# Perceiver block on one core: reordering the first maxima of cross attention

## Chip, cores, metric

One Trainium2 chip, one core. The metric is the device time of one execution in microseconds (us); lower is better.

## What is computed

Three residual layers on x (8 batches, 64 tokens, 512 features). The change touches only the first, cross attention to a context of 1601 tokens per batch:

```python
C_q  = layernorm(x) @ Wq_d                  # 512 tokens x 64
C_kv = ctx @ Wkv_d                          # per batch 1601 x 32 latents
q    = (C_q @ W_qk).reshape(b, n, 16, 32)   # 16 heads
scores = einsum('bnhl,bkl->bhnk', q, C_kv) / sqrt(32)
out = einsum('bhnk,bkhd->bnhd', softmax(scores), (C_kv @ Wv_u).reshape(b, k, 16, 32))
x = x + out
```

The second layer is an attention of 32 heads over gathered cache blocks, the third a gated feed-forward layer whose weights are first quantised. Both come after the cross attention and are not changed.

## The kernel before

Every engine has its own instruction stream; semaphores order them. The streams of the cross attention are written by hand, in order. TensorE is PE, VectorE DVE, ScalarE ACT, GpSimd POOL, and SyncE (SP) issues most transfers.

**Data.** `c_t` holds, for each of three batches in flight, the compressed context with latents on partitions: rows 0 to 31 the rounded high part, 32 to 63 the low part (value minus high), 64 to 95 the high part again. `q_t` holds the queries as high, high, low, so that one matmul over 96 rows gives a product of split precision. A "pair" is two matmuls into two neighbouring PSUM banks (402 keys each): `max_scores(b, i)` makes pair i of batch b (16 pairs: 8 tiles of 128 query rows by two halves of the keys), `take_max(b, i)` on DVE takes the maximum over both banks. After all 16, `negate_max` and `turn_max` put the negated maxima into a row of `q_t`; the scores are then made a second time, transposed (`scores`), exponentiated by ACT (`exponential`), multiplied with the latents (`values`) and summed by POOL (`add_pair`).

**Prologue (0 to 51 us).** The layer norm, the queries of token tiles 0 to 3, the compression of batch 0 (bank 4) and of batch 1 (bank 3), and the 16 maxima of batch 0, for which nothing can run ahead. PE's order is: `compress(0)`, `latent_queries(1)` (C_q of tiles 1 to 3), `natural(0)` (four transposes of batch 0's latents, which wait for DVE's copy `c_parts`), `queries(1)`, then pairs 0 to 15. Behind pairs 2 to 6 stands a chunk of `compress(1)`, behind pair 7 `natural(1)`, behind pairs 8 and 11 `queries(2)` and `queries(3)`.

ACT, in `first_keys`, copies `c_high`, places five pieces of the high part in `c_t`, and copies that part of 32x1601 a second time into rows 64 to 95 (L928, "doubling"). Only then comes `latent_copied(1)`, on which `queries(1)` waits; then the copies of queries 1, the exponential's table and `compressed(1)`, `compressed_high(1)`, and the copies of queries 2 and 3.

DVE subtracts the five low pieces (semaphore `s_kl`, one for each), copies `c_parts`, takes maximum 0, then `place_values(0)` (two copies out of `natural(0)`'s bank), then the maxima 1 to 15, with `place_values(1)` behind maximum 8.

POOL subtracts the low parts of queries 1, makes `c_low` of batch 1, subtracts those of queries 2 and 3 (L613, when ACT's copies L918 are there), fills the row of ones, and goes on to the batches: differences of feed-forward weights (L548), sums of probabilities (L555), and `c_low` of later batches (L569). ACT's exponentials of tile t wait until POOL and PE have read one of four buffers.

SP, in `place_keys(1)`, copies `c_high` and `c_low` of batch 1 by 15 transfers into `c_t`; `max_scores(1, 0)` waits for all of them. In the queue they stand behind the loads of context 2 and of six pieces of feed-forward weights. At the end of the cross attention SP gathers cache blocks and then loads the last weight pieces.

**Banks.** The first pairs of every batch use:

```python
def max_bank(i):
    if i < 2:
        return (6, 4)[i]
    return (4, 6)[i % 2]
```

So pairs 0, 1, 2, 3, 4 use banks 6, 4, 4, 6, 4. Pair 2 waits until maximum 1 is done (`s_max` 2), each later pair i until maximum i - 2 is.

Of the kernel before, what the change touches and what calls it, by code (L numbers as in the profile page):

```python
# [17 lines left out]
ACT = mybir.ActivationFunctionType  # L18
# [13 lines left out]
XH, LQ, LKV, XHD = 16, 64, 32, 32  # L32
NCTX = 1601
# [5 lines left out]
GROUPS = P // LKV  # L39
PER_GROUP = FULL // GROUPS  # L40
MAIN = PER_GROUP * P
SHIFT = 3 * LKV
# [27 lines left out]
def wait(eng, sem, count):  # L70

    if isinstance(count, int) and count <= 0:
        return
    eng.wait_ge(sem, count)
# [241 lines left out]
PIECE_AT = (0, 400, 800, NCTX - PIECE_KEYS)  # L316
PAIRS = PIECES // 2
MAXIMA = PAIRS * QTILES
# [24 lines left out]
CONTEXT_AT = {2: (0,), 3: (1,), 4: (2,), 5: (3,), 6: (DC,)}  # L343


def max_bank(i):


    if i < 2:
        return (6, 4)[i]  # L350
    return (4, 6)[i % 2]


# [8 lines left out]
def cross_attention(core, w, own):  # L362
# [15 lines left out]
    ones, c_nat, c_t, max_row, q_t, wv_u = (w[k] for k in ("ones", "c_nat", "c_t", "max_row", "q_t", "wv_u"))  # L378
# [42 lines left out]
    s_kh = core.sem("first_keys_high_done", own)  # L421
    s_kl = core.sem("first_keys_low_done", own)
# [3 lines left out]
    s_max = core.sem("max_part_done", own)  # L426
# [59 lines left out]
    with nc.Block() as block:  # L486
# [145 lines left out]
        def _(pe):  # L632
            def compress(b, parts=range(DC + 1)):
                bank = COMPRESS_BANK[b]
                if parts[0] == 0:
                    if b == 1:
                        pe.wait_ge(s_cqsb, 2)
                    elif b == 2:
                        pe.wait_ge(s_max, MAXIMA * (b - 1) + 1)
                    elif b > 2:  # L640
                        pe.wait_ge(s_max, MAXIMA * (b - 1) - 1)
                    if b > 0:
                        pe.wait_ge(s_ctx[b % 2], 16 * (b // 2 + b % 2))
                for c in parts:
                    if b == 0 and c < DC:
                        pe.wait_ge(s_ctx0[c], 16)
                    for g in range(GROUPS if c < DC else 0):
                        pe.matmul(psum[g * LKV:(g + 1) * LKV, bank, 0:MAIN], w["wkv_d"][:, c, :],
                                  ctx_t[b % 2][:, c, g * MAIN:(g + 1) * MAIN], start=(c == 0), stop=(c == DC - 1))
                if parts[-1] == DC:  # L650
                    for c in range(DC):
                        for g in range(GROUPS):
                            mm = pe.matmul(psum[g * LKV:(g + 1) * LKV, bank, MAIN:C_WIDTH], w["wkv_d"][:, c, :],
                                           ctx_t[b % 2][:, c, FULL * P:NCTX], start=(c == 0), stop=(c == DC - 1))
                    mm.then_inc(s_c, 1)

            def natural(b):
                bank = NATURAL_BANK[b]
                pe.wait_ge(s_cp, b + 1)
                if b == 1:  # L660
                    pe.wait_ge(s_cnat, 1)
                for i in range(PER_GROUP):
                    pe.transpose(psum[:, bank, i * P:(i + 1) * P], c_parts[:, i * P:(i + 1) * P], core.ident[:, :])
                pe.transpose(psum[0:TAIL, bank, MAIN:MAIN + LKV], c_parts[0:LKV, MAIN:C_WIDTH],
                             core.ident[0:LKV, 0:LKV]).then_inc(s_nat, 1)

            def max_scores(b, i):
                qt, pair = divmod(i, PAIRS)
                bank = max_bank(i)
                if i == 0 and b == 0:  # L670
                    pe.wait_ge(s_kl, GROUPS + 1)
                    pe.wait_ge(s_kh, GROUPS + 2)
                elif i == 0:
                    pe.wait_ge(s_ct, 16 * C_COPIES * b)
                if i == 0:
                    pe.wait_ge(s_qhi, 2 * (b // 2 + 1))
                    pe.wait_ge(s_qlo[b > 1], 2 * (b // 2 if b > 1 else 1))
                    wait(pe, s_shift, b)
                elif i == 1 and b == 0:
                    pe.wait_ge(s_cp, 1)  # L680
                elif i == 1 and b == 1:
                    pe.wait_ge(s_max, MAXIMA - 1)
                elif i == 1:
                    pe.wait_ge(s_d, 2 * (b - 1))
                elif i == 3 and b == 1:
                    pe.wait_ge(s_cnat, 3)
                elif i == 3 and b > 1:
                    pe.wait_ge(s_mix, b - 1)
                else:
                    pe.wait_ge(s_max, MAXIMA * b + (2 if i == 2 else i - 1))  # L690
                for k in range(2):
                    at = PIECE_AT[2 * pair + k]
                    mm = pe.matmul(psum[:, bank + k, 0:PIECE_KEYS],  # L693
                                   q_t[0:SHIFT, b, 2 * qt:2 * qt + 2, :].rearrange("p h n -> p (h n)"),
                                   c_t[0:SHIFT, b % 3, at:at + PIECE_KEYS], start=True, stop=True)
                mm.then_inc(s_sa, 1)
# [68 lines left out]
            def latent_queries(k):  # L765

                a, b = ((0, 1), (1, TT))[k]
                pe.wait_ge(norm.s_exact, b)
                pe.wait_ge(s_wq, 2 * 16)
                for c in range(DC):  # L770
                    for r in range(2):
                        mm = pe.matmul(psum[r * LQ:(r + 1) * LQ, LATENT_BANK[k], 0:(b - a) * P], wq_d[:, c, :],
                                       xn_t[:, c, a * P:b * P], start=(c == 0), stop=(c == DC - 1))
                mm.then_inc(s_cq, 1)

            def queries(j):

                pe.wait_ge(s_cqsb, 1 if j == 0 else 2)
                if j == 0:
                    pe.wait_ge(s_twice, 2)  # L780
                if j == 1:
                    pe.wait_ge(s_qhi, 2)
                    pe.wait_ge(s_qlo[0], 2)
                elif j == 2:
                    pe.wait_ge(s_qraw, 1)
                elif j == 3:
                    pe.wait_ge(s_cp, 2)
                    pe.wait_ge(s_cnat, 2)
                for h in range(0, XH // 2, 2):
                    for r in range(2):  # L790
                        rows = slice(r * LQ, (r + 1) * LQ)
                        mm = pe.matmul(psum[:, QUERY_BANK[j] + r, h // 2 * P:(h // 2 + 1) * P],
                                       w_qk[rows, h:h + 2, :, :], cq_t[rows, j * P:(j + 1) * P], start=True, stop=True)
                mm.then_inc(s_q, 1)
# [7 lines left out]
                norm.tile_turn(pe, j)  # L802
            compress(0)
            latent_queries(1)
            natural(0)
            queries(1)
            for i in range(MAXIMA):
                max_scores(0, i)
                if i in CONTEXT_AT:
                    compress(1, CONTEXT_AT[i])  # L810
                if i == 7:
                    natural(1)
                if i in QUERIES_AT:
                    queries(QUERIES_AT[i])
# [45 lines left out]
        def _(act):  # L860
# [42 lines left out]
            def latent_copied(k):  # L903
                a, b = ((0, P), (P, TOK))[k]
                act.wait_ge(s_cq, k + 1)
                act.activation(cq_t[:, a:b], psum[:, LATENT_BANK[k], 0:b - a], ACT.Copy).then_inc(s_cqsb, 1)
# [14 lines left out]
            def first_keys():  # L921

                act.wait_ge(s_c, 1)
                act.activation(c_high[:, :], psum[:, COMPRESS_BANK[0], 0:C_WIDTH], ACT.Copy).then_inc(s_chi, 1)
                for rows, bank, cols, keys in key_pieces():
                    act.activation(c_t[0:LKV, 0, keys], psum[rows, bank, cols], ACT.Copy).then_inc(s_kh, 1)
                act.wait_ge(s_kh, GROUPS + 1)
                act.activation(c_t[2 * LKV:SHIFT, 0, 0:NCTX], c_t[0:LKV, 0, 0:NCTX], ACT.Copy).then_inc(s_kh, 1)  # L928

            act.dma_start(wq_d[:, :, :], arg["Wq_d"].rearrange("p (c q) -> p c q", c=DC)).then_inc(s_wq, 16)  # L930
            act.dma_start(w_qk_in[:, :, :], arg["W_qk"].rearrange("q (h l) -> q h l", l=LKV)).then_inc(s_wq, 16)
# [5 lines left out]
            for j in range(1, TT):  # L937
                norm.tile_exact(act, j)
            first_keys()
            latent_copied(1)  # L940
            queries_high(1)
            queries_copied(1)
            act.wait_ge(s_rest, 1)
# [28 lines left out]
        def _(dve):  # L972
            def take_max(b, i):
                qt, pair = divmod(i, PAIRS)
                bank = max_bank(i)
                dve.wait_ge(s_sa, MAXIMA * b + i + 1)
                if i == 0:
                    wait(dve, s_neg, b)
                dve.tensor_reduce(max_part[:, qt, pair:pair + 1], psum[:, bank:bank + 2, 0:PIECE_KEYS],  # L979
                                  AX.XY, ALU.max).then_inc(s_max, 1)  # L980
# [73 lines left out]
            dve.tensor_copy(c_parts[:, :], psum[:, COMPRESS_BANK[0], 0:C_WIDTH]).then_inc(s_cp, 1)  # L1054
            for i in range(MAXIMA):
                take_max(0, i)
                if i == 0:
                    place_values(0)
                if i == 8:
                    place_values(1)  # L1060
# [920 lines left out]
```

## Time and profile before

| what | value |
|---|---|
| three runs | 909.49, 909.55, 912.41 us; median 909.55 us |
| the profiled execution | 912.59 us, of which its span is 910.7 us |
| PE busy | 866.1 us, 95% of the span |

The profile shows one execution. A row of the timeline gives start and duration in us from the span's start, engine, source line, output and input tiles, shapes and a count; in brackets stands the idle time of that engine ahead of it and what ended it. PEclk, and the column after the busy times in a row of stretches, is the clock granted to TensorE, 1.00 being 2.4 GHz and 0.50 being 1.2 GHz.

### The profile page before, as it was taken

The page shows a single profiled execution, that of the slowest core. Times are in us where ns is not written, and L with a number is a line of the kernel's source. Part 1 is how long each engine was busy: PE and PEld are TensorE (multiplying, and loading weights), DVE is VectorE, ACT ScalarE, POOL GpSimd, SP SyncE. Part 2 cuts the span into 40 slices and gives each one's busy share as a digit, 9 for nine tenths or more (in the row PEclk, how much of TensorE's full clock was granted, in tenths as well). Part 3 has the DMA queues.
Part 4 walks back from the last instruction along what each step waited for, and adds up shares of the span by engine and source line. Part 5 has one row for each costly group of instructions (what it writes and reads, how often), then busy time and mean ns, then how long its engine had stood idle before and what let it go on. Part 6 is the DMA issues. An engine that isn't in the chain of part 4 may idle for free.

```text
span 910.7 us, 15512 instructions
## 1 busy us (share of the span) xinstructions
PE 866.1 (95%) x5402; PEld 656.5 (72%) x5402; DVE 609.3 (67%) x994; ACT 521.5 (57%) x1010; POOL 416.2 (46%) x272
## 2 busy tenths in 40 slices
PE   6789999999997989999999999999999999899998
PEld 4444555455442668888888888888888887788886
DVE  4665666576551538858587585876858769768884
ACT  4555666666674547636366373763637647555552
POOL 2397887788876015424244242442424524154430
PEclk9979999999998889999999999999999999999999
DMA  9747664623660721102011020110202003445531
GB/s 365 273 173 290 234 244 145 257 89 113 186 202 1 277 82 47 47 1 70 23 46 46 0 69 23 48 44 8 72 12 67 14 1 113 165 139 189 197 101 47
DMA packets 43202, 102.96 MB, mean 113 GB/s; under 512 B 7954, under 2 KB 13074, under 8 KB 42258
## 3 DMA queue, kind: packets, MB, share of 16 engines
q1 hardware_dynamic: 42866, 102.06, 32.6%
q8 instruction: 30, 0.49, 0.2%
q10 hardware_dynamic: 288, 0.26, 0.1%
q14 instruction: 18, 0.15, 0.1%
HBM read 96.95 MB, written 1.05 MB: 108 GB/s over the span
## 4 chain that ended last, share of the span: by engine, by line
PE 60%; DVE 2%; ACT 1%; DMA 1%; POOL 0%; SPq 0%; issue 0%
PE psum L1356 11%; PE psum L1342 10%; PE psum L1472 8%; PE psum L1410 8%; PE psum L1368 6%; PE psum L1486 4%; PE psum L1395 3%; PE psum L1386 3%; PE psum L1391 3%; PE psum L1377 1%; PE psum L1387 1%; PE psum L1389 1%; DMA ffn_raw<-in_L_ffn_mean_w_dram 1%; POOL ffn_quant L1857 0%; DVE x L1828 0%; DVE norm_stats L162 0%
## 5 line engine op out<-in xcount | busy, mean ns | idle before, releaser
L1844 POOL TENSOR_TENSOR head_probs<-head_probs,inverse_den 128x576 f32<-128x576 f32 x128 | 147.3, 1151 | 273.2 <-DVE inverse_den L1697 273.1
L979 DVE TENSOR_REDUCE max_part<-psum 128x1 f32<-128x804 f32 x128 | 121.2, 990 | 48.3 <-PE psum L693 48.2
L869 ACT ACTIVATE probs<-psum 128x512 f32<-128x512 f32 (+1 forms) x208 | 107.8, 601 | 56.5 <-PE psum L714 48.6
L1579 ACT ACTIVATE head_probs<-psum,neg_max 128x576 f32<-128x576 f32 x128 | 94.7, 740 | 51.2 <-DVE neg_max L1710 50.4
L555 POOL TENSOR_TENSOR prob_sums<-probs 128x1024 f32<-128x1024 f32 x48 | 114.0, 2383 | 19.5 <-ACT probs L869 10.5
L1710 DVE TENSOR_REDUCE neg_max<-psum 128x1 f32<-128x576 f32 x128 | 96.9, 757 | 23.9 <-PE psum L1356 22.7
L1356 PE MATMUL psum<-k_high,query_t_high 128*128 (+1 forms) x256 | 86.7, 339 | 2.0 <-DVE coeff L1783 2.0
L1690 DVE TENSOR_TENSOR probs_t_low<-psum,probs_t_high 128x512 fp32r<-128x512 f32 x124 | 84.8, 684 | 1.0
L714 PE MATMUL psum<-q_t,c_t 97*128 97x512 f32 (+1 forms) x208 | 74.2, 437 | 8.7 <-ACT probs L869 7.0
L693 PEld LDWEIGHTS psum<-c_t,q_t 96*128 96x128 f32 x256 | 43.9, 191 | 50.9 <-DVE max_part L979 29.3
L693 PE MATMUL psum<-c_t,q_t 96*128 96x402 f32 x256 | 75.0, 376 | 5.6 <-DVE max_part L979 3.9
L1368 PE MATMUL psum<-ident,head_probs 128*128 128x128 f32 x496 | 77.9, 273 | 1.6 <-DVE query_t_low L1669 1.4
L1857 POOL TENSOR_TENSOR ffn_quant<-ffn_raw 128x1536 f32<-128x1536 f32 x13 | 45.6, 3508 | 67.6 <-DVE ffn_w_low L1774 26.9
L1356 PE MATMUL psum<-k_high,query_t_low 128*128 (+1 forms) x256 | 76.2, 298 | 0.0
L1356 PE MATMUL psum<-k_low,query_t_high 128*128 (+1 forms) x256 | 76.1, 297 | 0.0
L1585 ACT ACTIVATE probs_t_high<-psum 128x512 fp32r<-128x512 f32 x124 | 72.9, 588 | 0.5 <-PE psum L1377 0.5
L1368 PEld LDWEIGHTS psum<-ident,head_probs 128*128 128x128 f32 x496 | 60.6, 140 | 11.4 <-issue 2.2
L714 PEld LDWEIGHTS psum<-q_t,c_t 97*128 97x128 f32 (+1 forms) x208 | 38.4, 192 | 32.1 <-ACT probs L869 23.0
L1593 ACT ACTIVATE wo_t_high<-wo_nat 128x512 fp32r<-128x512 f32 x32 | 20.0, 626 | 72.4 <-PE psum L1410 72.4
L727 PE MATMUL psum<-probs,c_nat 128*32 128x512 f32 (+1 forms) x416 | 61.0, 621 | 0.0
L1752 DVE TENSOR_TENSOR x<-psum,x 128x512 f32<-128x512 f32 x32 | 22.1, 690 | 46.0 <-PE psum L1410 46.0
L548 POOL TENSOR_TENSOR w_raw<-w_raw 128x896 f32<-128x896 f32 x24 | 50.5, 2105 | 4.3 <-DMA w_raw<-in_L_ffn_mean_w_dram 4.3
(221 smaller groups left out, 1924.3 us busy)
## 6 DMA issues: line engine op xcount, KB each, us to landing
ctx_t_odd<-in_ctx_dram SPq DMA_DIRECT2D x4, 3202.0 KB, 10.7
w_raw<-in_L_ffn_w_dram SPq DMA_DIRECT2D x24, 448.0 KB, 5.3
w_raw<-in_L_ffn_mean_w_dram SPq DMA_DIRECT2D x24, 448.0 KB, 6.4
ffn_raw<-in_L_ffn_w_dram SPq DMA_DIRECT2D x42, 256.0 KB, 3.9
ffn_raw<-in_L_ffn_mean_w_dram SPq DMA_DIRECT2D x42, 256.0 KB, 4.2
cache<-in_ctx_dram SPq DMA_DIRECT2D x3, 3202.0 KB, 10.6
wq_nat<-in_L_attn_wq_dram SPq DMA_DIRECT2D x32, 256.0 KB, 2.9
wo_nat<-in_L_attn_wo_dram SPq DMA_DIRECT2D x32, 256.0 KB, 2.7
```

The costliest lines, as they stand in the source:

```text
L555: pool.tensor_tensor(sums[u][:, :], prob_buffer(b, 2 * u)[:, :], prob_buffer(b, 2 * u + 1)[:, :], ALU.add).then_inc(s_add, 1)
L693: mm = pe.matmul(psum[:, bank + k, 0:PIECE_KEYS], q_t[0:SHIFT, b, 2 * qt:2 * qt + 2, :].rearrange("p h n -> p (h n)"), c_t[0:SHIFT, b % 3, ...
L714: pe.matmul(psum[0:rows_of(t), n % SCORE_BANKS, :], lhs, rhs[:, half * BANK:(half + 1) * BANK], start=True, stop=True).then_inc(s_sb, 1)
L869: act.activation(prob_buffer(b, t)[0:rows, half * BANK:(half + 1) * BANK], psum[0:rows, n % SCORE_BANKS, :], ACT.Exp, scale=XSCALE).then_i ...
L979: dve.tensor_reduce(max_part[:, qt, pair:pair + 1], psum[:, bank:bank + 2, 0:PIECE_KEYS], AX.XY, ALU.max).then_inc(s_max, 1)
L1342: mm = pe.matmul(psum[:, head_bank(i), :], wq_t[a][:, c, :], (xh, xl)[b][:, c, :], start=(k == 0), stop=(k == 3 * DC - 1))
L1356: mm = pe.matmul(psum[:, bank, 0:HALF], q_t[a][:, qt * P:(qt + 1) * P], (k_high, k_low)[b][:, keys], start=(step == 0), stop=(step == 2))
L1368: mm = pe.transpose(bank[:, t * P:(t + 1) * P], probs[:, qt, t * P:(t + 1) * P], core.ident[:, :])
L1579: act.activation(probs[:, qt, :].rearrange("p (a k) -> p a k", a=2), psum[:, 2 * (qt % 2):2 * (qt % 2) + 2, 0:HALF], ACT.Exp, bias=neg_max ...
L1690: dve.tensor_tensor(probs_t[1][:, 0:ST, qt * P:(qt + 1) * P], psum[:, turn_bank(qt), :].rearrange("p (t q) -> p t q", t=ST), probs_t[0][:, ...
L1710: dve.tensor_reduce(neg_max[:, qt:qt + 1], psum[:, 2 * (qt % 2):2 * (qt % 2) + 2, 0:HALF], AX.XY, ALU.max, negate=True).then_inc(s["max"], 1)
L1844: pool.tensor_tensor(probs[:, qt, :], probs[:, qt, :], rden[:, qt:qt + 1].to_broadcast([P, KEYS]), ALU.mult).then_inc(s["norm"], 1)
```

## The change

Four things, all in the prologue.

1. For batch 0 all pairs alternate banks 6 and 4, so pair 2 shares banks with pair 0 and waits for maximum 0 alone (`s_max` 1). The last pair now sits in bank 4, hence the wait of `max_scores(1, 1)` for all 16 maxima.
2. ACT copies the latents' queries (`latent_copied(1)`) before the doubling, and doubles in two halves: columns 0 to 801, then 802 to 1600. Pair 0 waits for the first half and three of the five low pieces (keys 0 to 1151; it reads 0 to 801); pair 1 waits for the second half.
3. On PE, `natural(0)` moves from ahead of `queries(1)` to behind pair 1.
4. On DVE, `place_values(0)` moves from behind maximum 0 to behind maximum 2.

```diff
-def max_bank(i):
+def max_bank(b, i):
-    if i < 2:
-        return (6, 4)[i]
+    if b == 0 or i < 2:
+        return (6, 4)[i % 2]
     return (4, 6)[i % 2]
...
             def max_scores(b, i):
                 qt, pair = divmod(i, PAIRS)
-                bank = max_bank(i)
+                bank = max_bank(b, i)
                 if i == 0 and b == 0:
-                    pe.wait_ge(s_kl, GROUPS + 1)
+                    pe.wait_ge(s_kl, GROUPS - 1)
                     pe.wait_ge(s_kh, GROUPS + 2)
...
                 elif i == 1 and b == 0:
+                    pe.wait_ge(s_kh, GROUPS + 3)
                     pe.wait_ge(s_cp, 1)
                 elif i == 1 and b == 1:
-                    pe.wait_ge(s_max, MAXIMA - 1)
+                    pe.wait_ge(s_max, MAXIMA)
...
-                    pe.wait_ge(s_max, MAXIMA * b + (2 if i == 2 else i - 1))
+                    pe.wait_ge(s_max, MAXIMA * b + (2 if i == 2 and b > 0 else i - 1))
...
             latent_queries(1)
-            natural(0)
             queries(1)
             for i in range(MAXIMA):
                 max_scores(0, i)
+                if i == 1:
+                    natural(0)
...
                 act.wait_ge(s_kh, GROUPS + 1)
-                act.activation(c_t[2 * LKV:SHIFT, 0, 0:NCTX], c_t[0:LKV, 0, 0:NCTX], ACT.Copy).then_inc(s_kh, 1)
+                latent_copied(1)
+                for cols in (slice(0, 2 * PIECE_AT[1] + 2), slice(2 * PIECE_AT[1] + 2, NCTX)):
+                    act.activation(c_t[2 * LKV:SHIFT, 0, cols], c_t[0:LKV, 0, cols], ACT.Copy).then_inc(s_kh, 1)
...
             first_keys()
-            latent_copied(1)
             queries_high(1)
...
             for i in range(MAXIMA):
                 take_max(0, i)
-                if i == 0:
+                if i == 2:
                     place_values(0)
```

(`PIECE_AT[1]` is 400, `GROUPS` 4; `take_max` calls `max_bank(b, i)` too.)

## Rows read from the trace of the kernel before

**Rows 1.** The page: busy time of the engines and PE's granted clock by fortieths.
```profile
PE 866.1 (95%) x5402; PEld 656.5 (72%) x5402; DVE 609.3 (67%) x994; ACT 521.5 (57%) x1010; POOL 416.2 (46%) x272
...
PEclk9979999999998889999999999999999999999999
```

**Rows 2.** Timeline, 19 to 30 us: start, duration, engine, line, tiles, count, idle before.
```profile
19.29 2.80 PE L772 MATMUL psum<-xn_t,wq_d 128*64 128x384 f32 x16
...
22.01 1.54 ACT L928 ACTIVATE c_t<-c_t 32x1601 fp32r<-32x1601 f32 x1
...
23.57 0.49 ACT L906 ACTIVATE cq_t<-psum 128x384 f32<-128x384 f32 x1
...
23.62 0.55 PE L663 MATMUL psum<-ident,c_parts 128*128 128x128 f32 x3 [1.53 <-DVE c_parts L1054]
...
24.27 1.16 PE L792 MATMUL psum<-cq_t,w_qk 64*128 64x128 f32 x16
...
25.36 0.99 PE L693 MATMUL psum<-c_t,q_t 96*128 96x402 f32 x4
...
26.03 0.99 DVE L979 TENSOR_REDUCE max_part<-psum 128x1 f32<-128x804 f32 x1 [2.46 <-PE psum L693]
26.94 0.55 DVE L992 COPY c_nat<-psum 128x384 f32<-128x384 f32 x1
...
27.50 0.98 DVE L979 TENSOR_REDUCE max_part<-psum 128x1 f32<-128x804 f32 x1
...
28.54 0.64 PE L693 MATMUL psum<-c_t,q_t 96*128 96x402 f32 x2 [2.19 <-DVE max_part L979]
...
29.10 0.85 PE L648 MATMUL psum<-ctx_t_odd,wkv_d 128*32 128x384 f32 x8
...
29.89 0.63 PE L693 MATMUL psum<-c_t,q_t 96*128 96x402 f32 x2
```

**Rows 3.** Groups of instructions with shapes kept apart, 18 to 51 us.
```profile
L926 ACT ACTIVATE c_t<-psum 32x384 fp32r<-32x384 f32 x4 | 1.9, 478 | 0.1
```

**Rows 4.** Timeline of the later maxima, and two half-clock stretches with their granted clock.
```profile
34.10 0.63 PE L693 MATMUL psum<-c_t,q_t 96*128 96x402 f32 x2
...
43.70 3.70 DVE L979 TENSOR_REDUCE max_part<-psum 128x1 f32<-128x804 f32 x4 [0.58 <-PE psum L693]
...
30.44:33.85 3.41, 3.41 (x19) 0.90 (x18) 1.88 (x2) 0.67 (x2) 3.41 (x2) 0.50 1.04 296
...
47.50:57.74 10.24, 8.81 (x34) 5.47 (x38) 8.32 (x9) 4.73 (x8) 10.04 (x5) 0.50 0.85 329
```

**Rows 5.** Timeline and waits around the first scores of batch 0, all engines.
```profile
41.86 2.04 ACT L918 ACTIVATE prob_sums<-psum 32x1024 f32<-32x1024 f32 x2
...
44.07 9.29 POOL L613 TENSOR_TENSOR q_t<-prob_sums,q_t 32x1024 fp32r<-32x1024 f32 x4 [4.88 <-ACT prob_sums L918]
...
61.05 1.15 POOL L569 TENSOR_TENSOR c_low<-c_parts,c_high 128x449 fp32r<-128x449 f32 x1 [0.20 <-ACT c_high L883]
...
68.64 7.07 POOL L555 TENSOR_TENSOR prob_sums<-probs 128x1024 f32<-128x1024 f32 x3
...
PE psum L714 <- ACT probs L869: 1.3, 2, 0.9
```

**Rows 6.** DMA issues with their time to landing, and issues of the key copies.
```profile
ctx_t_odd<-in_ctx_dram SPq DMA_DIRECT2D x1, 3202.0 KB, 19.6
...
37.93 3.09 SPq L481 DMA_DIRECT2D c_t<-c_high  x4
...
47.40 0.59 SPq L483 DMA_DIRECT2D c_t<-c_low  x1
...
52.99 0.87 PE L693 MATMUL psum<-c_t,q_t 96*128 96x402 f32 x2
```

**Rows 7.** SyncE's and GpSimd's timeline at the start of the last batch.
```profile
234.36 0.36 SPq L284 DMA_DIRECT2D cache<-in_L_attn_k_cache_dram  x1
...
264.84 2.09 POOL L548 TENSOR_TENSOR w_raw<-w_raw 128x896 f32<-128x896 f32 x1 [4.27 <-DMA w_raw<-in_L_ffn_mean_w_dram]
```

More of the change, by code:

```diff
@@ L974, in take_max @@
                 qt, pair = divmod(i, PAIRS)
-                bank = max_bank(i)
+                bank = max_bank(b, i)
                 dve.wait_ge(s_sa, MAXIMA * b + i + 1)
```

## The prediction

> **What bounds the kernel now.** I read the page first. PE is busy 95% of the span, and the places where it is not, or where its clock is low, are few; the first three fortieths, which hold the prologue, are among them [rows 1]. The chain that ended last runs through PE in nearly all of its length. So a microsecond taken from the prologue counts in full if PE's stream behind it can follow, and that is the question.
>
> Then the timeline of the prologue, for what ends each wait. Three things hold up the maxima of batch 0 [rows 2]. ACT makes the 1.54 us doubling before the 0.49 us copy of the latents' queries, though PE had delivered those at 22.09 (19.29 + 2.80); `queries(1)` starts only at 24.27, behind `natural(0)`, and pair 0 at 25.36. Next, DVE puts the placing of the values between maxima 0 and 1, so maximum 1 starts at 27.50. Then pair 2, which shares its banks with pair 1, waits for that maximum: PE stands idle for 2.19 us until 28.54. Soon after that the clock falls to half for 3.41 us [rows 4].
>
> Last, what follows the prologue, in the timeline and the waits of batch 0. POOL begins its low parts of queries 2 and 3 at 44.07, when ACT's copy of queries 2 (41.86 + 2.04 = 43.90) is there, and is then busy almost without a gap until 75.71 (68.64 + 7.07). Its one wait in between that I use is 0.20 us at 61.05, for ACT's `c_high` of batch 2, which comes from PE. PE waits 1.3 us in all behind ACT, where ACT waits for POOL to free buffers [rows 5]. Here POOL sets the time and PE is hardly ahead of it, so both must move for the end to move.
>
> **The change, part by part.** All starts are those of the trace; hand-overs between engines take 0.06 us (maximum 1 ends at 27.50 + 0.98 = 28.48, pair 2 starts at 28.54) [rows 2].
>
> *Latents first, `natural(0)` away.* The latents' copy starts at 22.15 and ends at 22.64. `queries(1)` starts at 22.70, and the next instruction of PE can follow 1.09 us later (24.27 to 25.36) [rows 2]: pair 0 at 23.79 in place of 25.36, 1.57 us earlier. The weaker wait on the low pieces costs and gives nothing, because DVE's low pieces are done before pair 0 in either order.
>
> *Doubling in halves.* A 384-column copy takes 0.48 us [rows 3] and the 1601-column one 1.54 [rows 2], which makes 0.87 ns for a column and 0.84 us for each half. The first half runs 22.64 to 23.48, under `queries(1)`, with 0.3 us to spare. The second ends at 24.32. Pair 1 could start at 23.79 + 0.56 (the pitch of a pair, 28.54 to 29.10 [rows 2]) = 24.35 and starts at 24.38. A second instruction costs ACT about 0.14 us (0.84 twice against 1.54), and ACT has `queries(1)` to wait for anyway. If a half took as long as the whole, pair 0 would slip by 0.4 us; if the halves cost nothing extra, nothing changes. Bounds 0 and -0.4.
>
> *Banks alternate, two steps moved.* Maximum 0 starts 0.67 us after its pair (25.36 to 26.03) [rows 2], at 24.46, and ends at 25.45. `natural(0)`, whose first three and last transposes take 0.65 us (23.62 to 24.27), now stands behind pair 1 and fills 24.94 to 25.59; so it is nearly free, since pair 2 could not start before 25.51. Pair 2 starts at 25.59 in place of 28.54: **2.95 us earlier**. A chunk of `compress(1)` takes 0.79 (29.10 to 29.89) [rows 2]; its context lands at 4.30 + 19.6 = 23.9, before it is wanted at 26.15 [rows 6]. Pair 3 starts at 26.94, pair 4 at 28.29, pair 5 at 29.64, by 1.35 us each.
>
> DVE's pitch of maxima is 0.92 us (four in 3.70, the last 0.99 long [rows 4]): maxima 1 and 2 start at 25.38 and 26.30, the values' placing at 27.22, maximum 3 at 27.78 (placing 0.56, from 26.94 to 27.50 [rows 2]). It ends at 28.77, and pair 5, which needs it, comes at 29.64. So the moved placing is hidden behind the chunks of compression; without those it would cost its 0.56 again. What waits for it is `natural(1)`, behind pair 7, far off. The order of ACT's later copies is unchanged.
>
> *The clock.* Before, from pair 3 to pair 5 passed 4.21 us (29.89 to 34.10) [rows 2, 4] where two steps of 1.35 make 2.70: **1.51 us** go to the stretch at half clock, 1.2 GHz, which began after an idle gap of 2.19 us. After the change PE has no gap over 0.1 us from 22.70 on, by the steps above. I take this stretch as gone: pair 5 moves by 34.10 - 29.64 = 4.46 us, that is 2.95 + 1.51. Bounds for this term: 0 and 1.51.
>
> The Trainium skill (TensorE: Matmul & The Clock Gate, "What's actually happening") says that the window in which activity is judged runs freely and does not start with the kernel. By that rule the 1.51 us need not be in every execution before, and the sum for an execution without it would be 2.95.
>
> *From pair 5 to the scores.* Here nothing is edited. The last four maxima are one block on DVE (43.70 to 47.40 [rows 4]) and move by 4.46 as well. POOL's start at 44.07 hangs on `queries(2)` behind pair 8 and moves with it, to 39.61. The rank of waits stays: POOL's stream to 75.71 sets the time.
>
> *Batch 0.* PE runs at half clock from 47.50 to 57.74 [rows 4], around the thin work of the turned maxima. That thin place remains and the low stretch with it, but where it lies against the work is open. PE has no margin where POOL waits for `c_high` (0.20 us at 61.05), so if PE comes later there, POOL does too; if it comes earlier, at most 0.2 us is won, since POOL binds. I take 0.2 us off. Bounds: +0.2, and -1.7 for a low stretch longer by the 3.41 us of the other one, at half speed.
>
> *Transfers.* `place_keys(1)` is issued 37.93 to 47.99, and pair 0 of batch 1 at 52.99 needs it [rows 6]. It moves 4.46 earlier, to 33.47, when the weight loads are still in flight. At worst the transfers land as late as before, 47.99 plus some 2 us (the pace of their issue bounds it from below), against a need at 48.53: PE waits 1.5 us, of which 1.3 are the PE margin against POOL [rows 5]. I take nothing; bound -0.3 to -1.5.
>
> The Trainium skill (DMA: Bandwidth & Descriptors, "Queues, rings and completion order") says that each DMA engine takes descriptors in ring order. By that rule the early key copies do stand behind the weights, and the sum would be smaller by up to that bound.
>
> *The other batches.* They repeat their own periods. The last batch starts on POOL behind a weight transfer (264.84 after 4.27 us of waiting), which follows the gather begun at 234.36 [rows 7]; the gather in turn is released by the batch before it, so this chain moves too.
>
> **Sum.** 2.95 + 1.51 - 0.2 = 4.3 us. The profiled execution took 912.59 us in all (1.89 outside its span), and becomes 908.3. It lies 3.0 us above the median of the runs shown; the median becomes 909.55 - 4.3 = **905.3 us**.
>
> **Rivals.**
>
> 1. *Order alone.* The low stretch at 30 us is absent from the executions that make the median, or another takes its place. For it: the runs shown spread over 3 us with one program, which something of this kind must explain. Against: the idle gap of 2.19 us stands in every execution, by dependencies. 909.55 - 2.95 = 906.6.
> 2. *Given back in batch 0.* PE gets through `compress(2)` later against POOL, by 1.7 us of half clock or 1.5 us of waiting for the keys. 4.3 - 1.6 = 2.7, or 1.1 with both: 906.9 to 908.5. For it: the margin of 0.20 us. Against: a stretch of 10.24 us is already paid.
> 3. *It does not arrive.* A chain of its own, such as transfers, fixes the end of the cross attention: 909.5. For it: POOL waits 4.27 us for a transfer in the last batch. Against: that chain starts from work of batch 5.
> 4. *Slower.* The half clock in batch 0 becomes longer. Each 3.41 us more costs PE 1.7. To pass 912.3 it has to eat 4.3 and then 2.7 more: over 14 us of added low clock beyond what stands at 47.50 to 57.74. Price 912.5 or more. PE is dense from 53 us on, which speaks against it.
> 5. *More.* The later drops of the clock, in the middle of the span [rows 1], fall better as well: one stretch of 3.41 us fewer gives 1.7, so 903.6.
>
> **How the numbers follow.** My forecast 0.50 (its own range 904.7 to 906.0), rival 1 0.18, rival 2 0.13, rival 3 0.07, rival 4 0.04, rival 5 0.08. A change of 0.3% (2.7 us) is about what a measurement of this kernel can tell from none. Faster by more: forecast, rival 5 and nearly all of rival 1 (906.6 is just below 906.8), with a tenth of rival 2: 0.50 + 0.08 + 0.17 + 0.01 = 0.76. Slower 0.04. Within: 0.20. Range 903.4 to 908.4: it leaves out rivals 3 and 4 and the ends of 2 and 5.
>
> **What would show it.** Pair 0 at about 23.8 and pair 2 at 25.6, with no idle PE between; the placing of values between maxima 2 and 3; granted clock 1.00 from 24 to 40 us; POOL's run of low parts starting near 39.6; the last maximum ending near 42.9; PE's first scores near 46 to 46.5; then the same rows as before in the batches, 4.3 earlier. Wrong would be: PE idle at pair 1 for the second half; a half-clock stretch before 35 us; POOL waiting over 1 us for `c_high` of batch 2, or pair 0 of batch 1 waiting for key copies.

## The result: 4.7 to 5.8 us faster, a little more than forecast

In 12 runs each, the changed kernel takes 903.75 us in the median (901.39 to 905.64) and the kernel before 908.81 (905.17 to 914.0). The ratio is 0.9936 with a 95% interval of 0.9919 to 0.9952, which is 5.8 us less, 4.4 to 7.4. (The medians above are 5.1 us apart; the ratio on record is not their quotient, 0.9944, but holds it in its interval.) Measured a second time the ratio is 0.9948 (0.9931 to 0.9964), 4.7 us less, 3.3 to 6.3. The forecast was 4.3 us less, 905.3 us: right in sign, but just short of the first interval. The time measured lies below the range of the forecast itself (904.7 to 906.0), just inside the wide one (from 903.4), and nearest to the price of rival 5, 903.6.

The page of the changed kernel, by the same two rows as [rows 1]:

```profile
PE 861.6 (96%) x5402; PEld 654.4 (73%) x5402; DVE 609.3 (68%) x994; ACT 521.6 (58%) x1011; POOL 416.4 (46%) x272
...
PEclk9989999999998989999999999999999999999999
```

Its timeline of all engines, for [rows 2, 4, 5] (start, duration, engine, line, tiles, count, idle time before):

```profile
18.00 2.80 PE L773 MATMUL psum<-xn_t,wq_d 128*64 128x384 f32 x16
...
20.91 0.49 ACT L908 ACTIVATE cq_t<-psum 128x384 f32<-128x384 f32 x1 [0.23 <-PE psum L773]
21.43 1.63 ACT L932 ACTIVATE c_t<-c_t 32x802 fp32r<-32x802 f32 x2
...
21.46 1.16 PE L793 MATMUL psum<-cq_t,w_qk 64*128 64x128 f32 x16 [0.66 <-ACT cq_t L908]
...
22.55 1.21 PE L694 MATMUL psum<-c_t,q_t 96*128 96x402 f32 x4
...
23.22 2.80 DVE L982 TENSOR_REDUCE max_part<-psum 128x1 f32<-128x804 f32 x3 [0.96 <-PE psum L694]
...
24.27 0.64 PE L694 MATMUL psum<-c_t,q_t 96*128 96x402 f32 x2
...
25.94 0.55 DVE L995 COPY c_nat<-psum 128x384 f32<-128x384 f32 x1
...
26.50 0.98 DVE L982 TENSOR_REDUCE max_part<-psum 128x1 f32<-128x804 f32 x1
...
28.32 0.63 PE L694 MATMUL psum<-c_t,q_t 96*128 96x402 f32 x2
...
37.91 3.70 DVE L982 TENSOR_REDUCE max_part<-psum 128x1 f32<-128x804 f32 x4 [0.58 <-PE psum L694]
...
38.28 9.29 POOL L613 TENSOR_TENSOR q_t<-prob_sums,q_t 32x1024 fp32r<-32x1024 f32 x4 [4.88 <-ACT prob_sums L920]
...
41.94 2.02 PE L702 MATMUL psum<-ident,max_row 128*97 128x128 f32 x8 [1.45 <-DVE max_row L988]
...
55.32 1.14 POOL L569 TENSOR_TENSOR c_low<-c_parts,c_high 128x449 fp32r<-128x449 f32 x1 [0.27 <-ACT c_high L885]
```

Read it from the projection of the latents' queries (18.00; before 19.29). That start differs by 1.29 us for a reason outside the change. The first input was used 0.45 us earlier (3.92 against 4.37), the transposes behind it took 2.59 us in place of 2.82, and `compress(0)` took 2.79 in place of 3.39, first before and then after:

```profile
15.51 3.39 PE L648 MATMUL psum<-cache,wkv_d 128*32 128x384 f32 x32
```

```profile
14.83 2.79 PE L648 MATMUL psum<-cache,wkv_d 128*32 128x384 f32 x32
```

So subtract the start everywhere. Pair 0 starts 4.55 us behind the projection, before 6.07 [rows 2]: 1.52 gained, forecast 1.57. DVE takes three maxima in a row from 23.22, then places the values at 25.94. Pair 2 starts 6.27 behind, before 9.25: 2.98 gained, forecast 2.95. Pair 5 (28.32) is 10.32 behind, before 14.81 [rows 4]: 4.49, forecast 4.46. PE has no bracket, that is no idle gap, between 21.46 and pair 5. POOL's part (38.28) and the last four maxima (37.91) moved by the same 4.50, and POOL's wait for `c_high` at 55.32 is 0.27 us, as before within 0.07.

Two stretches of it, with the granted clock in the third column from the right:

```profile
20.00:42.00 22.00, 18.06 (x159) 10.09 (x155) 18.74 (x27) 17.34 (x22) 9.56 (x5) 1.00 0.96 324
42.00:60.00 18.00, 16.80 (x116) 9.50 (x117) 11.40 (x13) 9.54 (x18) 17.53 (x9) 0.72 0.55 205
```

From 20 to 42 us the clock is 1.00 throughout: the stretch at half clock near 30 us is gone. In the second row it is 0.72, from the stretch at half clock from 41.8 to 52.1 us that replaced the one from 47.50 [rows 4].

### The profile page after: what moved, and what is told of

It reads as the page before. It is cut to its first block, busy times and chain, and to the rows that moved or that the text cites. A ratio compares the mean times of both kernels' runs of the same rounds, so it can differ in the third digit from the quotient of the medians.

```text
span 901.8 us, 15515 instructions
## 1 busy us (share of the span) xinstructions
PE 861.6 (96%) x5402; PEld 654.4 (73%) x5402; DVE 609.3 (68%) x994; ACT 521.6 (58%) x1011; POOL 416.4 (46%) x272
## 4 chain that ended last, share of the span: by engine, by line
PE 61%; DVE 2%; ACT 1%; DMA 1%; POOL 0%; SPq 0%; issue 0%
PE psum L1359 11%; PE psum L1345 10%; PE psum L1475 9%; PE psum L1413 8%; PE psum L1371 6%; PE psum L1489 4%; PE psum L1398 3%; PE psum L1389 3%; PE psum L1394 3%; PE psum L1380 1%; PE psum L1392 1%; PE psum L1390 1%; DMA ffn_raw<-in_L_ffn_mean_w_dram 1%; POOL ffn_quant L1860 0%; DVE x L1831 0%; DVE norm_stats L162 0%
## 5 line engine op out<-in xcount | busy, mean ns | idle before, releaser
L548 POOL TENSOR_TENSOR w_raw<-w_raw 128x896 f32<-128x896 f32 x24 | 50.7, 2111 | 3.6 <-DMA w_raw<-in_L_ffn_mean_w_dram 3.5
```

## The experiments

The start of that projection varies between executions, 16.75 to 19.29 us, whatever the kernel. Inputs are not the main reason: in the profiles that start at 18.20 us or earlier `compress(0)` takes 2.79 us, in those from 18.84 on 3.18 to 3.56. In the traces the first record of full clock comes at 11.63 us where the start is 16.75 and at 16.79 where it is 19.29, so a clock that rises late at the very start would explain it; no run tested that. The table therefore gives, for one profile of each kernel, the distance from that projection (128x384) to the start of maximum 5 and to PE's first matmul for the denominators of batch 0, both in us, and the half-clock stretches before 70 us. The ratio to the kernel before, with its interval, comes from the timed runs.

| kernel | max 5 | denominators | half clock | ratio |
|---|---|---|---|---|
| before | 15.48 | 67.38 | 30.4-33.9, 47.5-57.7 | |
| before, again | 16.79 | 69.15 | 28.4-35.3, 48.9-59.2 | 1.0005 (0.9986-1.0024) |
| before, third | 13.95 | 65.60 | 42.3-52.6 | |
| before, fourth | 15.46 | 67.25 | 29.8-33.2, 46.8-57.1 | |
| after | 10.99 | 62.93 | 41.8-52.1 | 0.9936 (0.9919-0.9952) |
| after, again | 11.06 | 62.70 | 39.6-49.8 | 0.9948 (0.9931-0.9964) |
| early start only | 15.43 | 67.81 | 25.8-32.7, 46.3-56.5 | 0.9986 (0.9968-1.0004) |
| banks only | 12.49 | 64.52 | 43.0-53.2 | 0.9977 (0.9957-0.9996) |
| before, gap filled | 13.95 | 65.59 | 42.8-53.1 | 0.9982 (0.9960-1.0004) |
| after, values back | 11.67 | 64.02 | 42.5-52.8 | 0.9938 (0.9925-0.9950) |
| after, one doubling | 11.47 | 63.55 | 44.2-54.5 | 0.9956 (0.9935-0.9976) |
| after, gap | 17.63 | 70.14 | 27.1-37.3, 51.0-61.2 | 1.0009 (0.9992-1.0026) |
| after, gap filled | 14.04 | 66.40 | 47.2-57.4 | 0.9981 (0.9962-1.0000) |
| after, matrix later | 10.99 | 63.01 | 43.5-53.8 | 0.9959 (0.9946-0.9972) |
| after, warm | 10.98 | 64.14 | 47.6-54.4 | 0.9952 (0.9934-0.9970) |
| warm, ones early | 10.99 | 65.75 | 50.7-57.5 | 0.9979 (0.9964-0.9993) |
| warm, ones early, matrix later | 10.99 | 62.84 | 55.4-62.2 | 0.9947 (0.9927-0.9968) |
| warm, ones early, matrix at end | 10.98 | 61.60 | 46.3-49.7 | 0.9945 (0.9924-0.9966) |

### The two halves of the change

Early start alone takes parts 2 and 3 of the change, with `max_bank`, the wait of pair 2 and `place_values(0)` as before.

> Only the earlier start: latents' queries first, the doubling in halves, natural order behind pair 1; the banks and the place of the values as before. My sum: pair 0 starts 1.57 us earlier against the latent projection's end, maximum 0 ends at the equivalent of 25.45, the values are placed, maximum 1 follows, and pair 2 starts 1.56 us earlier than before. PE still idles about 1.4 us before pair 2. If the idle gap of 2.2 us was what brought the half clock near 30 us, it may or may not come with 1.4: gain 1.6 without the clock term, 3.1 with it. Rival (a start fixed by something else, a transfer): gain 0.

Banks alone is the rest:

```diff
-    if i < 2:
+    if b == 0 or i < 2:
...
-                if i == 0:
+                if i == 2:
                     place_values(0)
```

> Only the banks alternate and the values are placed behind maximum 2; the start as before. My sum: pair 0 as before, pair 2 starts when maximum 0 ends, 27.08 by the trace of before in place of 28.54, so 1.4 to 1.5 us earlier. PE idles 0.7 us before it. Gain 1.4 if the half clock near 30 us stays, 2.9 if it goes. Rival (the placing of the values holds later maxima back): gain under 1.

Pair 2 of the early start, on PE's timeline, and its stretch of half clock:

```profile
24.82 0.64 PE L694 MATMUL psum<-c_t,q_t 96*128 96x402 f32 x2 [1.64 <-DVE max_part L982]
...
25.80:32.70 6.90, 6.90 (x34) 2.11 (x30) 3.04 (x4) 1.82 (x3) 4.67 (x2) 0.51 1.03 352
```

Pair 2 of the kernel with banks alone:

```profile
24.91 0.64 PE L693 MATMUL psum<-c_t,q_t 96*128 96x402 f32 x2 [0.73 <-DVE max_part L979]
```

Pair 2 starts 7.90 us behind the projection in the first (24.82 - 16.92) and 7.77 in the second (24.91 - 17.14), against 9.25 before: 1.35 and 1.48 gained, and both together 2.98 in the changed kernel. They nearly add up (2.83). But PE still stands idle for 1.64 us in the first, half clock follows 1.0 us after pair 2 starts, and at maximum 5 nothing is left of the gain. In the second the gap is 0.73 us and none follows in this profile. The two ratios, 1.3 and 2.1 us of gain, have intervals too wide to tell them apart.

### The clock

Seven unused matmuls behind pair 1 of the kernel before, and nothing else:

```diff
                 max_scores(0, i)
+                if i == 1:
+                    for _ in range(7):
+                        pe.matmul(psum[:, 3, 0:PIECE_KEYS], ..., c_t[0:SHIFT, 0, 0:PIECE_KEYS], start=True, stop=True)
```

> The kernel before, with seven more matmuls of 96x402 into bank 3 behind pair 1, whose results nobody reads, so that PE works in the gap of 2.2 us and nothing else moves. Clock theory: the half clock near 30 us is gone and with it 1.5 us, gain 1.5. Rival (the stretch of half clock is chance, or hidden behind other waits): gain 0, or a loss of 0.2 where the fill runs over the gap.

```profile
23.89 1.46 PE L811 MATMUL psum<-c_t,q_t 96*128 96x402 f32 x7
26.24 0.64 PE L693 MATMUL psum<-c_t,q_t 96*128 96x402 f32 x2 [0.89 <-DVE max_part L983]
...
28.94 0.63 PE L693 MATMUL psum<-c_t,q_t 96*128 96x402 f32 x2
```

The fill (L811) leaves 0.89 us of the 2.19 us gap, pair 2 stays where it was (9.23 behind the projection), no half clock comes before 42 us, and pair 4 follows at the pace of 1.35 us for each. The measured ratio is 1.6 us of gain, with an interval that just reaches zero. The mean granted clock of the timed runs, which the record has for each of them, says the same with less doubt: 0.9849 in the 12 runs with the fill, 0.9815 in the 35 of the kernel before beside them. Read as time at half clock, (1 - 0.9849) x 2 x 905 us, that is 27 against 34 us in a run.

The kernel before was profiled three more times.

> The kernel before against itself, for how far two sets of its runs differ and how its half-clock stretches and its start vary between executions. Ratio 1.000; if the extra in the changed kernel's result came from a start 1.3 us earlier and from shorter half-clock stretches after 275 us by chance, this profile too will show other values there than the first one did.

> The kernel before, a third profile. Clock theory: half clock begins within 4 us of pair 2's idle gap, for 3.41 or 6.83 us, and the distance from the projection of the latents' queries to the denominators of batch 0 is 67.4 us with one step, about 69 with two. Chance theory: in some profile there is none, and the distance is 65.8.

> As the third profile of the kernel before: half clock behind the gap for 3.41 or 6.83 us; distance 67.4 or 69 us.

The second profile of the kernel before, and the third with its pair 2:

```profile
28.40:35.30 6.90, 6.90 (x34) 2.12 (x30) 3.02 (x4) 1.60 (x3) 4.68 (x2) 0.51 1.00 313
```

```profile
25.99 0.64 PE L693 MATMUL psum<-c_t,q_t 96*128 96x402 f32 x2 [2.19 <-DVE max_part L979]
...
20.00:42.00 22.00, 16.94 (x152) 9.90 (x152) 16.12 (x22) 14.35 (x17) 7.85 (x4) 1.00 0.92 323
```

So with the same gap of 2.19 us, of four executions one had 6.83 us of half clock behind it, two had 3.41, and one had none. Against the third, whose maximum 5 comes at 13.95 like that of the filled kernel, the others lose 1.5 us with one step and 2.8 with two, and at the denominators 1.7 and 3.6. My expectation that every profile would have one fell; it was made from two profiles. The Trainium skill (TensorE: Matmul & The Clock Gate, "What's actually happening") says that the window of the clock's monitor runs freely, so the placing varies from run to run. By that rule the stretch need not be the same each time; the traces agree, with 0, 3.41, 3.41 and 6.83 us.

The converse, in the changed kernel: pair 2 waits for ACT's copies of queries 1, with a bare gap and with ten unused matmuls in it.

```diff
+                elif i == 2 and b == 0:
+                    pe.wait_ge(s_max, 1)
+                    pe.wait_ge(s_qraw, 1)
```

> The changed kernel with one more wait: pair 2 waits for ACT's copies of queries 1 (which end at 27.21 in the trace after), so PE idles about 2.9 us between natural order and pair 2 where it had no gap. Clock theory: the direct loss is 3.0 us up to pair 2, and a half-clock stretch of one or two steps of 3.41 us follows within 4 us of the gap and costs another 1.5 to 2.8, so 4.5 to 5.8 later than the changed kernel at maximum 5 and after. Rival (a low stretch is chance): 3.0 later, no stretch.

> The same wait, but ten more matmuls of 96x402 into bank 3 stand ahead of it, whose results nobody reads, so PE works through the gap. Clock theory: 3.0 us later than the changed kernel at maximum 5, with the granted clock at 1.00 up to 40 us. The difference to the kernel with the bare gap is the price of the clock alone, 1.5 to 2.8 us. Rival: both the same.

Pair 2 of the kernel with the bare gap, and its stretch:

```profile
28.56 1.01 PE L697 MATMUL psum<-c_t,q_t 96*128 96x402 f32 x2 [3.11 <-ACT prob_sums L923]
...
27.10:37.30 10.20, 8.74 (x36) 2.82 (x40) 4.02 (x6) 2.79 (x4) 4.67 (x2) 0.50 1.01 333
```

The same stretch with the gap filled:

```profile
27.10:37.30 10.20, 9.03 (x92) 4.13 (x92) 6.81 (x9) 3.72 (x6) 5.68 (x3) 1.00 1.02 345
```

The filled kernel is 3.05 us later than the changed one at maximum 5 (14.04 against 10.99), as expected. The fill does not close the gap: 1.06 us of it are left. The bare gap costs 3.59 us more there and 3.74 at the denominators. Its half clock is 10.2 us long, one step of 3.41 more than I allowed, and begins at 27.1, inside the gap. In time the ratios differ by 0.0028, 2.5 us, but their intervals overlap. The mean granted clock of the ten timed runs each is 0.9811 with the bare gap and 0.9854 with the filled one, 34 against 26 us at half clock. The work is the same but for the fill, so it is the idle time of PE that brings the half clock here. In the profiles it costs 3.7 us on top of the wait, in the times 2.5 with a wide margin.

The gaps ahead of pair 2 can be ranked over the profiles. Behind 0.73 us (banks only), 0.89 (before, gap filled) and 1.06 (after, gap filled) no half clock came before 42 us; with 1.64 (early start only) it was 6.9 us, with 2.19 (before, four profiles) 0, 3.41, 3.41 and 6.83, with 3.11 (after, gap) 10.2. Most of these are single profiles, and no limit can be read from them.

### The small parts

> The changed kernel once more, for a second interval beside the first (0.9936, 0.9919 to 0.9952). The additive account (2.96 us of order, 1.6 us of clock, the mean of what the runs with filled and unfilled gaps gave) makes 4.6 us, ratio 0.9950. A further cause in the change would keep it at 0.9936 or lower. In the profile no half clock between 20 and 40 us; the later stretches, after 270 us, elsewhere than in the first profile.

It came out at 0.9948, near the 0.9950 of the sum and inside the first interval.

Values back puts `place_values(0)` behind maximum 0 again.

```diff
-                if i == 2:
+                if i == 0:
                     place_values(0)
```

> The changed kernel with the placing of the values back behind maximum 0. Maximum 1 then ends 0.56 us later, and pair 3, which waits for it, is ready at 26.98 against 26.94 by my sum. So nothing: 0 to 0.2 us lost at maximum 5, ratio as the changed kernel. Rival (this move carries a large part of the gain): 0.5 us or more lost.

```profile
24.35 0.85 PE L648 MATMUL psum<-ctx_t_odd,wkv_d 128*32 128x384 f32 x8 [0.61 <-DMA ctx_t_odd<-in_ctx_dram]
```

The ratio is that of the changed kernel (0.9938). In the profile maximum 5 is 0.68 us later, but 0.61 of it is this wait: `compress(1)` waits for the context of batch 1 itself, which I had counted as landed well ahead. In this execution the projection started early (16.82) and the context landed at 24.3. The changed kernel has come within reach of that transfer. The wait also hides what the move itself would cost:

```profile
23.10 0.64 PE L694 MATMUL psum<-c_t,q_t 96*128 96x402 f32 x2
...
23.68 1.88 DVE L982 TENSOR_REDUCE max_part<-psum 128x1 f32<-128x804 f32 x2
```

Pair 3 could follow pair 2 by 1.35 us, at 24.45, but maximum 1 ends at 23.68 + 0.98 = 24.66. So pair 3 would come at 24.72, 0.27 us late, where my sum had 0.04. This is an estimate; no run shows it bare. At the denominators this profile is 1.09 us later (64.02 against 62.93), which the ratio does not confirm.

One doubling joins the two halves of ACT's copy, and pair 1's wait for the second half goes.

```diff
-                    pe.wait_ge(s_kh, GROUPS + 3)
...
-                for cols in (slice(0, 2 * PIECE_AT[1] + 2), slice(2 * PIECE_AT[1] + 2, NCTX)):
+                for cols in (slice(0, NCTX),):
```

> The changed kernel with the doubling in one instruction of 1.54 us behind the latents' copy. Pair 0 waits for all of it: the copy ends at 22.64 by the trace of before and the doubling at 24.18, so pair 0 starts at 24.24 in place of 23.79, 0.45 us later, pair 1 right behind it at 24.80 in place of 24.38. All later pairs 0.4 us later. Rival (the halves carry nothing, later waits absorb it): 0.

```profile
24.32 0.97 PE L693 MATMUL psum<-c_t,q_t 96*128 96x402 f32 x4 [0.45 <-issue]
```

PE stands 0.45 us before pair 0, and maximum 5 is 0.48 later (11.47 against 10.99). As expected; the ratios cannot resolve it.

### What binds in batch 0

The forecast held that POOL binds there and PE could win 0.2 us at most. Warm adds eleven unused matmuls (`keep_warm(n)` issues n of those of the fill, into bank 0):

```diff
+                if i in (13, 15):
+                    pe.wait_ge(s_qraw, 2)
+                    keep_warm({13: 2, 15: 5}[i])
             turn_max(0)
+            keep_warm(4)
```

> The changed kernel with eleven more matmuls into bank 0, whose results nobody reads: two behind pair 13, five behind pair 15, four behind the turned maxima. They fill PE's gaps from 38 to 45 us. If the half clock from 41.8 to 52.1 goes, PE's turned maxima take 1.1 us in place of 2.0 and its scores and compression of batch 2 come up to 5 us earlier. By my reading POOL binds from 38 to 68 us: the third sum of probabilities then ends no more than 0.3 us earlier, and the kernel gains 0.3 at most. Rival (PE binds in batch 0, through its low clock): gain 2 to 5 us.

DVE, then PE, then two stretches of the warm kernel:

```profile
41.30 1.21 DVE L1040 TENSOR_SCALAR diag<-ident,cos_col 128x128 f32<-128x128 f32 x1
42.43 2.41 DVE L1041 TENSOR_SCALAR swap<-swap,sin_col 128x128 f32<-128x128 f32 x1
44.88 2.37 DVE L1043 TENSOR_TENSOR rope<-diag,swap 128x128 f32<-128x128 f32 x1
...
47.61 1.90 DVE L991 TENSOR_REDUCE max_part<-psum 128x1 f32<-128x804 f32 x2
...
48.66 5.35 PE L648 MATMUL psum<-cache,wkv_d 128*32 128x384 f32 x32 [1.76 <-DVE max_part L991]
...
40.80:47.50 6.70, 4.85 (x23) 3.23 (x22) 6.55 (x7) 5.10 (x8) 6.58 (x4) 1.00 0.87 301
47.60:54.40 6.80, 5.74 (x56) 2.20 (x60) 1.90 (x3) 0.00 (x0) 6.72 (x3) 0.50 0.57 245
```

The fill does its work: 1.00 up to 47.5, and the first score comes 26.26 us behind the projection in place of 27.16. Then PE waits 1.76 us for maximum 0 of batch 1. On DVE that maximum stands behind the rotation matrix (41.30 to 47.6), whose 128x128 instructions take up to 2.4 us beside POOL's. The wait is itself a gap, the clock falls to half inside it, at 47.6, and the compression of batch 2 takes 5.35 us. The denominators are 1.2 us later than without the fill, and no gain is measured over the changed kernel. Neither POOL nor PE's clock alone explains that: a third engine holds PE.

With POOL's fill of the row of ones also moved ahead of the low parts of queries 2:

```diff
                     pool.wait_ge(s_clo, 1)
+                    pool.memset(c_t[SHIFT:STACK, 1:3, :].bitcast(F32), 1.0).then_inc(s_rest, 1)
+                    pool.wait_ge(s_rest, 5)
...
             pool.wait_ge(s_qlo[1], 2 * (TT - 1))
-            pool.memset(c_t[SHIFT:STACK, 1:3, :].bitcast(F32), 1.0).then_inc(s_rest, 1)
-            pool.wait_ge(s_rest, 5)
```

> As the kernel with eleven more matmuls, and POOL's fill of the row of ones (2.87 us, at 47.7 in the trace after) moves ahead of the low parts of queries 2, into POOL's idle time of 4.88 us. If POOL binds in batch 0, its stream is 2.9 us shorter where it counts; with PE early enough by the full clock, gain 2.5 to 3.0 against the changed kernel. If PE binds, the gain is that of the other kernel, whatever POOL does.

```profile
51.92 5.35 PE L648 MATMUL psum<-cache,wkv_d 128*32 128x384 f32 x32 [3.55 <-DVE max_part L991]
...
59.23 1.15 POOL L569 TENSOR_TENSOR c_low<-c_parts,c_high 128x449 fp32r<-128x449 f32 x1 [5.98 <-ACT c_high L894]
```

It is worse: 3.55 us of waiting, and POOL in turn stands 5.98 us for `c_high`. In this profile DVE's last step of the matrix, beside POOL's differences of the weights, took 1.79 us in place of 0.16. So the matrix was moved, first behind maximum 1 of batch 1 without any fill:

```diff
             negate_max(0)
-            rope_matrix()
...
                     elif i == 1:
+                        rope_matrix()
                         place_values(2)
```

> The changed kernel, with DVE's rotation matrix (six instructions, 41.8 to 48.1 us in the trace after) moved from behind the negated maxima to behind maximum 1 of batch 1, where DVE idles 5.7 us. With eleven fill matmuls PE waited 1.8 to 3.6 us for maximum 0 of batch 1, which stood behind that matrix. Without fills PE came to that point late by itself, at half clock: gain 0.0 to 0.3 us. Rival (DVE's matrix holds the changed kernel too): 1 us or more.

As forecast, nothing at the denominators (63.01 against 62.93). The ratio, 0.9959, shows no gain either and is if anything worse. With all three:

> All three together: fill matmuls, POOL's fill of the row of ones early, and DVE's rotation matrix later. If the waits seen one by one are all there are, PE compresses batch 2 at full clock and at once, near 45 to 48 us for a projection at 18.0, POOL's low part of batch 2 waits less than 0.5 us, POOL's third sum ends 2.9 us earlier than in the changed kernel, and the whole gains 2.5 to 3.0 us on it (ratio near 0.990 to the kernel before). If half clock comes back at compression, the gain shrinks to about 1.

```profile
47.48 2.79 PE L648 MATMUL psum<-cache,wkv_d 128*32 128x384 f32 x32
...
56.14 1.04 PE L694 MATMUL psum<-c_t,q_t 96*128 96x402 f32 x2 [2.09 <-DVE c_nat L1006]
```

The forecast of about 0.990 was missed (0.9947). Now the compression runs at once and at full speed (2.79 us at 47.48), but pair 2 of batch 1 waits 2.09 us for DVE, which is still at the matrix, and half clock comes at 55.4. The denominators come where they were. Last, the matrix at the end of batch 0:

```diff
             negate_max(0)
-            rope_matrix()
...
+                if b == 0:
+                    rope_matrix()
                 if b + 3 < BATCH:
                     place_values(b + 3)
```

> The changed kernel with fill matmuls, POOL's fill of the row of ones early, and DVE's rotation matrix at the end of batch 0, where DVE waits 5.4 us for natural order. Nothing is left on DVE between the maxima of batch 1, so PE compresses batch 2 at full clock near 29.5 us behind the projection and goes on. If POOL binds in batch 0: its third sum ends 2.9 to 3.1 us earlier than in the changed kernel and the whole gains 1.3 (PE's waits in batch 0) to 3 us, ratio 0.991 to 0.993. If PE binds by its clock, a half-clock stretch comes before 65 us all the same and the gain is 0 to 1.

```profile
45.37 0.63 PE L694 MATMUL psum<-c_t,q_t 96*128 96x402 f32 x2 [0.48 <-DMA c_t<-c_low]
...
46.30:49.70 3.40, 3.40 (x23) 1.13 (x25) 1.73 (x2) 1.06 (x2) 3.27 (x3) 0.50 1.07 460
```

POOL's third sum ends 45.96 us behind the projection, 1.3 earlier than in the changed kernel (47.29) and not the 2.9 to 3.1 that I expected, and the denominators come 1.3 earlier. Even here PE waits 0.48 us for the last key copy, and 3.4 us of half clock follow 0.9 us later; POOL waits 1.81 us for `c_high` again. The ratio of 0.9945 shows no gain over the changed kernel. No version measured beats it.

## Why the forecast came out as it did

*Latents first, doubling in halves: right.* 1.52 against 1.57 us, and with one doubling 0.48 us more at maximum 5, near the bound of 0.4 given for it.

*Banks and the two steps moved: right.* 2.98 against 2.95, and each half of the change gives half of it. That the values' placing is free behind maximum 2 is seen (no idle PE up to pair 5). What it would cost in its old place no run shows bare; 0.27 us by the estimate above, against 0.04 in my sum.

*The clock: the step that failed.* The mechanism was right and the term, 1.51 us, was too small. "Bounds for this term: 0 and 1.51" took one profiled execution for the upper end, and what the drops of the clock elsewhere would do stood at nothing in the sum (rival 5). Over four profiles of the kernel before the term is 0, 1.5, 1.5 and 2.8 us at maximum 5, up to 3.6 at the denominators. The mean distance to the denominators is (67.38 + 69.15 + 65.60 + 67.25) / 4 = 67.35 before and (62.93 + 62.70) / 2 = 62.8 after: 4.5 us. Of this 2.8 is the order (65.60 without any half clock at 30 us), 1.7 the clock. So the prologue gives 4.5 in place of 4.3, with a larger spread than I gave it.

Four profiles and two are few. The mean granted clock of the timed runs covers more: 0.9817 in the 96 runs of the kernel before beside the experiments, 0.9853 in the 18 of the changed kernel. As time at half clock this is 33.3 against 26.5 us, 6.8 less in a run. At half speed 6.8 us are worth at most 3.4 us, so the clock's whole share lies between the 1.7 of the profiles and 3.4. With 2.8 for the order that makes 4.5 to 6.2, which holds both results.

*The rest of the first result* (5.8 - 4.5 = 1.3, inside its interval) is thus likely clock as well, but where in the run I can't assign. From the denominators to the end the four profiles before take 820.2 to 824.1 us and the two after 819.3 and 820.8, and the other kernels of the table, unchanged there, 820.8 to 824.9; half-clock stretches between 261 and 338 us lie elsewhere in each. They sum to 13.7 to 20.5 us in the kernel before and to 13.7 in both profiles of the changed one, but also to 13.7 in two of the four before. That is as far as profiles go; whether the earlier arrival has a part in it stays open.

*From pair 5 to the scores, the other batches: right*, by 4.50 us at 38 us and 4.45 at the denominators (67.38 - 62.93).

*Batch 0: the low stretch stayed,* from 41.8, and POOL's wait at `c_high` was 0.27 us in place of 0.20. The 0.2 us taken off were not seen: POOL's `c_low` starts there 4.44 us earlier and the denominators 4.45, against 4.46 for pair 5 by my sum. "If it comes earlier, at most 0.2 us is won, since POOL binds" was wrong in its reason: DVE's rotation matrix held PE as soon as PE was faster. With it away, and POOL 2.9 us shorter, 1.3 us were won in the profile.

*Transfers: right for the key copies,* for which PE did not wait in the changed kernel; it did (0.48 us) once PE was faster still. Of the context of batch 1 I took the landing of one execution as ample, and it has since been waited for.

*Rivals.* Order alone is what an execution without half clock before would show; one in four did. Given back in batch 0, no arrival, and slower did not occur. *More* (903.6) is nearest to the 903.75 measured. The clocks of the timed runs agree with its condition, one stretch of 3.41 us fewer beyond the one at 30 us. That the stretch is missing in the middle of the span, where it looked for it, is not shown.

## What to carry to other kernels

An idle gap of PE can cost more than its length, because the clock may fall in it or behind it, and how much differs from one execution to the next; size such a term from several profiles and never from one, and look at the mean granted clock of all timed runs. Before pricing an engine's lead as lost to one rival, check all streams that it meets next: here each wait removed from PE showed another, on DVE, then on a transfer, and in each of those profiles the clock fell to half in the new gap or soon behind it. Compare traces from a common point of the work, because the start alone moved by 2.5 us.

## What the runs showed that was not expected

- The same kernel, with the same idle gap of 2.19 us, had 0, 3.41 or 6.83 us of half clock behind it, worth 0, 1.5 and 2.8 us.
- What sets the start of a half-clock stretch is open. In the warm kernel, with the work before it at 1.00, the clock fell about 0.7 us into a wait of 1.76 us.
- The same DVE instruction of the rotation matrix (128x128 in SBUF) took 0.28 us where POOL had just gone idle, 0.66 mostly beside POOL's fill of the row of ones, and up to 2.42 beside its sums of tensors. The last one, 128x1, took 0.16 us, or 1.68 to 1.97 where it stood beside POOL's differences of the weights or sums of probabilities; each of those three ended within 0.03 us of POOL's instruction.
